# Attention over four 32x32 images: one load queue, rows on other queues, values ahead of the first scores, a quartered end

## The chip, the cores and the metric

The kernel runs on one core of a Trainium2 chip. The metric is the device time of one execution in microseconds, the median of several. The engines are TensorE (PE in the views, its weight loads PEld), VectorE (DVE), ScalarE (ACT), GpSimd (POOL) and SyncE (SP), which only issues transfers here.

## The reference

For each of 4 images of 256 channels and N = 1024 pixels, a block of self-attention with a residual:

```python
xf = x.reshape(B, Cc, N)
q = jnp.einsum('oc,bcn->bon', Wq, xf) + bq[None, :, None]
k = jnp.einsum('oc,bcn->bon', Wk, xf) + bk[None, :, None]
v = jnp.einsum('oc,bcn->bon', Wv, xf) + bv[None, :, None]
scores = jnp.einsum('bqi,bqj->bij', q, k)
attn = jax.nn.softmax(scores, axis=-1)
out = jnp.einsum('bcj,bij->bci', v, attn)
return out.reshape(B, Cc, W, H) + x
```

q and k have 32 channels, v has 256. All is float32.

## The kernel before

Every float32 operand of a product is cut in two: a high part rounded to the format that TensorE reads fast (fp32r), and a low part, the rest. A product of two such operands is three products (high by high, high by low, low by high), which is how `x_hi`, `x_lo`, `wv_hi`, `w_hi`, `w_lo`, `v_hi`, `v_lo` come about. For q and k the parts are stacked on 96 partitions (`q_a`, `k_a`, and copies `q_b`, `k_b`), so one product with 96 rows does all three.

An image passes through four stages. *Projection*: q, k (`project_qk`), and v in 8 pixel tiles of 128 (`v_tile`, six products of 256 columns each). *Scores*: 8 tiles of 128x1024 (`scores`, two products of 512 columns), of which only the row maximum (VectorE, `row_max`) and the sum of exponentials (ScalarE, `sum_exp`) are used. From both comes the shift of each pixel, negative maximum less log of the sum (`shifts`), cut into two parts, transposed into a row by VectorE (`turn_shifts`), and moved by two small transfers (`send_rows`, one for the high and one for the low part) into partitions 96 and 97 of `q_b`; `k_b` has ones there. *Transposed scores*: with these rows, `scores_t` gives the shifted scores transposed, 128 keys by 512 queries, one product per tile; ScalarE's exponential of it (`exp`) is the finished weight, `w_full`. Its high part `w_hi` is made by ScalarE (a second exponential with rounded output) or by VectorE (`cut_w`), its low part `w_lo` by VectorE or GpSimd (`split_w`); `cut_by_act` and `split_by_pool` say by which, from the tile's number. *Weighted sum*: `weigh_v` adds six products of 512 columns per tile into `acc`, two blocks of 128 channels (c = 0, 1). After 8 key tiles one half of the queries (h) is done, and VectorE's `finish` adds bias and residual, channel block by channel block.

A turn of 16 steps (`turn`) does the weighted sums of one image: step s weighs tile s % 8 of half s // 8, while TensorE is two tiles ahead with `scores_t`. Between them the table `FRONT` places the projections and scores of the next image: scores at steps 6 to 13, values from step 5, the last values in step 15. The order on each engine is the order of the code; the engines wait for one another by counting semaphores. PSUM is full: `acc`, `st` (two transposed tiles) and two `slot`s that the front work shares.

The first image has its own start. TensorE runs `keep_busy` products on zeros (fillers) until the data are there, then `first_project_qk`, more fillers, the first four score tiles mixed with the value tiles, `first_rows` (the shifts of the first half turned into a row by products with an identity, `eye_r`, and copied into `q_b` by ScalarE's `put_first_rows`), and the first transposed scores. The homes of these tiles in PSUM are in `FIRST_HOME` and `FIRST_V`. The small weights and the second piece of the first image come over ScalarE's queue, the other loads over SyncE's.

The queues matter for what follows. GpSimd's loop goes through all tiles n; at n % 16 = 8 it issues `k_a` and `q_a` blocks of the next image and the rows of the second half (`send_rows(b, 1)`), at n % 16 = 13 the rows of the next image's first half, and only then subtracts:

```python
if n % PER == JT + 5 and more:
    send_rows(b + 1, 0)
split_w(n)
```

SyncE loads, sends the stacks (`second_stack`) and stores the results.

## Time and profile before

| | |
|---|---|
| median of 3 runs | 168.96 us (168.79 to 169.66) |
| profiled execution | 169.59 us, its span 167.7 us |
| TensorE | busy 160.9 us of the span (96%), 781 matmuls |
| VectorE | 139.1 us (83%) |
| ScalarE | 108.0 us (64%) |
| GpSimd | 47.2 us (28%) |
| transfers | 14.41 MB, 86 GB/s on average |

The span runs from the first recorded event to the last; the execution's own time has 1.9 us more around it. A matmul's recorded duration contains its way through the array, so that of two matmuls in a row overlaps; the distance between their starts is what one costs.

### The profile page before, as it was taken

How to read it: one execution, taken by the hardware profiler on the slowest of the kernel's cores; microseconds unless marked ns; L12 is line 12 of the kernel's file. 1: busy time of each engine (PE TensorE's matmuls, PEld its weight loads, DVE VectorE, ACT ScalarE, POOL GpSimd, SP SyncE). 2: the span in 40 equal slices, each digit the busy share in tenths (PEclk: the TensorE clock that was granted, in tenths of full speed). 3: DMA queues.
4: the chain of work that ended last, by engine and by line, in shares of the span. 5: the costliest groups of instructions: out<-in, count | busy, mean ns of one | idle time of the engine just before them, and what ended most of it. 6: DMA issues, size and time to landing. Idle time of an engine off the chain costs nothing. (4 is left out here: it accounts for less than half of the span.)

```text
span 167.7 us, 2420 instructions
## 1 busy us (share of the span) xinstructions
PE 160.9 (96%) x781; PEld 131.0 (78%) x781; DVE 139.1 (83%) x221; ACT 108.0 (64%) x198; POOL 47.2 (28%) x63
## 2 busy tenths in 40 slices
PE   7898999999999999999999999999999999999992
PEld 4566888797887898788787898788787898876880
DVE  1879889899979999899979998898989879855353
ACT  3667896855997665767896655746896555754410
POOL 4229830080335300340335300250335300203500
PEclk9999999999999999999999999999999999999999
DMA  5923357054311230152310230052310230003003
GB/s 146 390 88 95 68 233 250 0 125 114 127 49 25 69 125 0 34 139 66 125 49 16 83 125 2 16 144 78 124 52 8 89 125 0 4 1 125 0 0 125
DMA packets 7660, 14.41 MB, mean 86 GB/s; under 512 B 1512, under 2 KB 1696, under 8 KB 7648
## 3 DMA queue, kind: packets, MB, share of 16 engines
q1 hardware_dynamic: 6528, 13.11, 23.9%
q0 software_dynamic: 832, 0.82, 2.3%
q10 hardware_dynamic: 288, 0.33, 0.6%
q8 instruction: 6, 0.10, 0.2%
q14 instruction: 6, 0.05, 0.1%
HBM read 4.52 MB, written 4.19 MB: 52 GB/s over the span
## 5 line engine op out<-in xcount | busy, mean ns | idle before, releaser
L826 PE MATMUL acc<-w_hi,v_hi 128*128 128x512 f32 x128 | 51.2, 400 | 0.0
L826 PE MATMUL acc<-w_hi,v_lo 128*128 128x512 f32 x128 | 50.3, 393 | 0.0
L434 ACT ACTIVATE w_full<-st 128x512 f32<-128x512 f32 x64 | 37.8, 593 | 10.5 <-PE st L812 10.5
L401 ACT ACTIVATE dump<-slot,negmax 128x1024 f32<-128x1024 f32 x29 | 32.4, 1118 | 13.2 <-DVE negmax L554 12.9
L834 PE MATMUL acc<-w_lo,v_hi 128*128 128x512 f32 x120 | 38.7, 398 | 0.3 <-POOL w_lo L330 0.2
L609 DVE TENSOR_TENSOR w_lo<-w_full,w_hi 128x512 fp32r<-128x512 f32 x48 | 33.1, 692 | 5.9 <-ACT w_full L434 1.6
L554 DVE TENSOR_REDUCE negmax<-slot 128x1 f32<-128x1024 f32 x29 | 35.3, 1216 | 1.6 <-PE slot L746 1.6
L330 POOL TENSOR_TENSOR w_lo<-w_full,w_hi 128x512 fp32r<-128x512 f32 x16 | 20.7, 1294 | 46.6 <-ACT w_full L434 46.5
L826 PEld LDWEIGHTS acc<-w_hi,v_hi 128*128 128x128 f32 x128 | 24.2, 189 | 7.1 <-DVE x_sb L618 1.2
L826 PEld LDWEIGHTS acc<-w_hi,v_lo 128*128 128x128 f32 x128 | 24.2, 189 | 5.3
L834 PEld LDWEIGHTS acc<-w_lo,v_hi 128*128 128x128 f32 x120 | 22.3, 188 | 7.0 <-POOL w_lo L330 2.0
L812 PE MATMUL st<-q_b,k_b 98*128 98x512 f32 x64 | 25.4, 400 | 0.2 <-issue 0.2
L600 DVE CAST w_hi<-w_full 128x512 fp32r<-128x512 f32 x43 | 21.6, 503 | 4.8 <-ACT w_full L434 4.3
L431 ACT ACTIVATE w_hi<-st 128x512 fp32r<-128x512 f32 x21 | 12.4, 593 | 7.6 <-PE st L812 7.5
L686 PE MATMUL slot<-wv_hi,x_hi 128*128 128x256 f32 x60 | 16.8, 280 | 0.0
L686 PE MATMUL slot<-wv_lo,x_hi 128*128 128x256 f32 x60 | 16.8, 279 | 0.0
L686 PE MATMUL slot<-wv_hi,x_lo 128*128 128x256 f32 x60 | 16.7, 279 | 0.0
L746 PE MATMUL slot<-k_a,q_a 96*128 96x512 f32 x48 | 15.3, 401 | 0.0
L423 ACT ACTIVATE v_hi<-slot 128x512 fp32r<-128x512 f32 x12 | 7.2, 599 | 12.4 <-PE slot L686 12.4
L348 POOL DMA_DIRECT2D q_b<-shift_rows x14 | 8.1, 580 | 21.6 <-DVE shift_rows L582 21.6
L746 PEld LDWEIGHTS slot<-k_a,q_a 96*128 96x128 f32 x48 | 13.1, 310 | 1.4 <-issue 0.4
L812 PEld LDWEIGHTS st<-q_b,k_b 98*128 98x128 f32 x64 | 12.0, 188 | 2.0 <-issue 0.6
(83 smaller groups left out, 188.1 us busy)
## 6 DMA issues: line engine op xcount, KB each, us to landing
out<-x_sb SPq DMA_DIRECT2D x7, 512.0 KB, 2.8
x_sb<-x SPq DMA_DIRECT2D x3, 1024.0 KB, 5.9
k_b<-k_a SPq DMA_DIRECT2D x8, 192.0 KB, 2.5
q_b<-q_a SPq DMA_DIRECT2D x8, 192.0 KB, 2.7
x_sb<-x SPq DMA_DIRECT2D x3, 256.0 KB, 4.2
k_a<-qk_parts SPq DMA_DIRECT2D x12, 64.0 KB, 2.1
q_a<-qk_parts SPq DMA_DIRECT2D x12, 64.0 KB, 2.3
out<-x_sb SPq DMA_DIRECT2D x2, 256.0 KB, 2.1
```

What stands on the lines that cost most here:

```text
L330: nc.gpsimd.tensor_tensor(w_lo[:, r, :], w_full[:, r, :], w_hi[:, r, :].bitcast(fp32), ALU.subtract).then_inc(w_split_pool, 1)
L401: nc.scalar.activation(dump[:, t % 2, :], s_home(b, t), ACT.Exp, bias=negmax[:, t:t + 1], accum_out=rowsum[:, t:t + 1]).then_inc(rowsum_re ...
L431: nc.scalar.activation(w_hi[:, r, :], st[:, j % 2, :], ACT.Exp).then_inc(w_cut_act, 1)
L434: nc.scalar.activation(w_full[:, r, :], st[:, j % 2, :], ACT.Exp).then_inc(exp_done, 1)
L554: nc.vector.tensor_reduce(out=negmax[:, t:t + 1], in_=s_home(b, t), op=ALU.max, axis=AX.X, negate=True).then_inc(negmax_ready, 1)
L600: nc.vector.tensor_copy(w_hi[:, r, :], w_full[:, r, :]).then_inc(w_cut_dve, 1)
L609: nc.vector.tensor_tensor(w_lo[:, r, :], w_full[:, r, :], w_hi[:, r, :].bitcast(fp32), ALU.subtract).then_inc(w_split_dve, 1)
L686: last = nc.tensor.matmul(dst, lhs, rhs, start=(i == 0), stop=(i == len(terms) - 1))
L746: last = nc.tensor.matmul(s_home(b, t)[:, cols(h)], pixels(b, t), k_a[0:K_A, cols(h)], start=True, stop=True)
L812: nc.tensor.matmul(st[:, j % 2, :], k_b[0:K_B, j * P:(j + 1) * P], q_b[0:K_B, cols(h)], start=True, stop=True).then_inc(st_ready, 1)
L826: nc.tensor.matmul(acc[:, c, :], v[:, b % 2, j, ch], w_hi[:, r, :], start=(j == 0 and v is v_hi), stop=False)
L834: last = nc.tensor.matmul(acc[:, c, :], v_hi[:, b % 2, j, c * P:(c + 1) * P], w_lo[:, r, :], start=False, stop=(j == JT - 1))
```

## The change

Six edits in one. (1) All loads are issued by SyncE, the small weights first, then the four pieces of the first image. (2) The rows of the next image's first half are sent by SyncE instead of GpSimd; of the last image's second-half rows ScalarE sends the high part and GpSimd the low part. (3) In the first image GpSimd makes `w_lo` of tiles 3 and 5 (besides 9, 11, 13) and no longer of tile 0. (4) The first two value tiles are computed right behind the projections; their high part is cut by ScalarE, TensorE subtracts it in PSUM by a product with a negative identity, and ScalarE copies what is left as the low part. The other value tiles move up, and the scores of tile 4 ahead of the first transposed product. (5) In the last image the last two steps of each half take channel block 0 of both tiles first, then block 1. (6) In the last half of the last image channel block 1 is summed in two quarters (one in `acc`, one in `slot[0]`), finished and stored separately, one by ScalarE's queue.

```diff
     def split_by_pool(n):
-        return n % PER in (0, 9, 11, 13)
+        return n % PER in ((3, 5, 9, 11, 13) if n < PER else (0, 9, 11, 13))
...
-        FIRST_V = (slot[1][:, cols(1)], st[:, 1, :], slot[0][:, cols(0)], slot[0][:, cols(1)])
+        FIRST_V = (slot[1][:, cols(1)], slot[1][:, cols(1)], st[:, 1, :], slot[0][:, cols(0)])
...
+        def send_rows(engine, b, h, parts=(HI, LO), done=None):
+            engine.wait_ge(shift_turned, 2 * b + h)
+
+            if b:
+                engine.wait_ge(st_ready, PER * (b - 1) + JT * h + JT)
+            for part in parts:
+                engine.dma_start(
+                    q_b[SHIFT + part:SHIFT + part + 1, cols(h)].bitcast(fp32).rearrange("o (q n) -> o q n", n=P),
+                    shift_rows[part:P:SQUARE, h, :]).then_inc(done or row_in[h], DMA)
...
         @block.sync
         def _(sp):
-            for i in (0, 2, 3):
+            sp.dma_start(small_sb[:, :], small).then_inc(small_in, DMA)
+            for i in range(4):
                 c, part = piece(i)
                 sp.dma_start(x_sb[:, 0, c, part], x_v[0, :, c, part]).then_inc(x0_in[i], DMA)
...
                 second_stack(k_b, k_a, 0, kb_in[0])
+                send_rows(sp, b + 1, 0)
                 sp.wait_ge(st_ready, PER * b + PER)
...
-            for c in range(CT):
-                sp.wait_ge(acc_read, 4 * BATCH - 1 + c)
-                sp.dma_start(out_v[BATCH - 1, :, c, cols(1)], x_sb[:, BATCH - 1, c, cols(1)]).then_inc(out_sent[1], DMA)
+            sp.wait_ge(acc_read, 4 * BATCH - 1)
+            sp.dma_start(out_v[BATCH - 1, :, 0, cols(1)], x_sb[:, BATCH - 1, 0, cols(1)]).then_inc(out_sent[1], DMA)
+            sp.wait_ge(acc_read, 4 * BATCH + 1)
+            sp.dma_start(out_v[BATCH - 1, :, 1, quarter(3)], x_sb[:, BATCH - 1, 1, quarter(3)]).then_inc(out_sent[1], DMA)
...
-                    send_rows(b, 1)
+                    send_rows(pool, b, 1, (HI, LO) if more else (LO,))
                     if more:
                         second_blocks(b + 1, 1)
-                if n % PER == JT + 5 and more:
-                    send_rows(b + 1, 0)
                 split_w(n)
...
+            first_cut_v(0)
+            act.wait_ge(v0_rest_ready, 1)
+            nc.scalar.activation(v_lo[:, 0, 0:VT, :], v_home(0, 0).rearrange("p (j c) -> p j c", c=C),
+                                 ACT.Copy).then_inc(v_split, 1)
             for t in range(TH):
                 sum_exp(0, t)
             log_sums(0, 0)
-            first_cut_v(1)
+            first_cut_v(2)
+            first_cut_v(3)
             put_first_rows()
-            first_cut_v(2)
             exp(0)
-            first_cut_v(3)
             exp(1)
...
+                    before, t, image = front(b, s - 2)
+                    if before == S and t == JT - 1 and b + 1 == BATCH:
+                        send_rows(act, b, 1, (HI,), last_row_in)
...
+            def finish_last(i):
+                part = slice(HALF + i * QUARTER, HALF + (i + 1) * QUARTER)
+                if i == 0:
+                    dve.wait_ge(third_quarter_ready, 1)
+                else:
+                    dve.wait_ge(av_done, TILES)
+                nc.vector.scalar_tensor_tensor(
+                    out=x_sb[:, BATCH - 1, 1, part], in0=(slot[0] if i else acc[:, 1, :])[:, 0:QUARTER],
+                    scalar=bv_sb[:, 1:2], in1=x_sb[:, BATCH - 1, 1, part],
+                    op0=ALU.add, op1=ALU.add).then_inc(acc_read, 1)
...
-            split_v(0, 0)
             split_v(0, 1)
             split_v(0, 2)
             row_max(0, TH)
+            cut_w(0)
+            split_w(0)
             split_v(0, 3)
...
+            def weigh_last_tile(h, j, c):
+
+                b = BATCH - 1
+                if c == 0:
+                    weigh_ready(b, h, j)
+                for part, dst in places(h, c):
+                    weigh_high(b, h, j, c, dst, part)
+                    last = weigh_low(b, h, j, c, dst, part)
+                    if (h, j, c) == (1, JT - 1, 1) and part == quarter(0):
+                        last.then_inc(third_quarter_ready, 1)
+                if c:
+                    last.then_inc(av_done, 1)
+                elif j == JT - 1:
+                    last.then_inc(acc0_ready, 1)
...
-            keep_busy(13, QUARTER)
+            keep_busy(14, QUARTER)
             for i in range(4):
                 first_project_qk(i)
-            keep_busy(24, P)
+
+            pe.wait_ge(wv_split, 1)
...
+            for i, (t, xs, w, c) in enumerate(first_v):
+                last = nc.tensor.matmul(v_home(0, 0)[:, t * C:(t + 1) * C], xs[:, 0, c, px[t]], w[:, c, :],
+                                        start=(i == 0), stop=(i == len(first_v) - 1), skip_group_check=True)
+            last.then_inc(v_ready, 1)
+            keep_busy(8, P)
             for t in range(3):
                 first_scores(t)
-            pe.wait_ge(wv_split, 1)
-            v_tile(0, 0)
-            v_tile(0, 1)
+            pe.wait_ge(v_cut, 1)
+            pe.wait_ge(eye_cut, 1)
+            nc.tensor.matmul(v_home(0, 0), eye_r[:, :], v_hi[:, 0, 0:VT, :].rearrange("p j c -> p (j c)"),
+                             start=False, stop=True, skip_group_check=True).then_inc(v0_rest_ready, 1)
+            pe.wait_ge(v_split, 1)
+            v_tile(0, 2)
+            v_tile(0, 3)
             first_scores(3)
```

On ScalarE, between the cuts of the projections and the first exponentials of the scores, the order was this (`k_a`, `q_a` are the projected stacks, `dump` takes exponentials of which only the sum counts):

```order
L454 ACTIVATE q_a<-slot,small_sb 32x512 [waits qk_ready]
L401 ACTIVATE dump,rowsum<-acc,negmax 128x1024 [waits negmax_ready]
L401 ACTIVATE dump,rowsum<-st,negmax 128x1024 [waits negmax_ready]
L401 ACTIVATE dump,rowsum<-slot,negmax 128x1024 [waits rowsum_ready,negmax_ready]
L401 ACTIVATE dump,rowsum<-acc,negmax 128x1024 [waits rowsum_ready,negmax_ready]
L406 ACTIVATE logsum<-rowsum 128x4 [waits rowsum_ready]
L415 ACTIVATE v_hi<-st 128x512 [waits v_ready]
L411 ACTIVATE q_b<-st 2x512 [waits row_ready]
```

In the changed kernel it is this, on the same engine at the same place:

```order
L461 ACTIVATE q_a<-slot,small_sb 32x512 [waits qk_ready]
L422 ACTIVATE v_hi<-slot 128x512 [waits v_ready]
L474 ACTIVATE v_lo<-slot 128x512 [waits v0_rest_ready]
L407 ACTIVATE dump,rowsum<-acc,negmax 128x1024 [waits negmax_ready]
L407 ACTIVATE dump,rowsum<-st,negmax 128x1024 [waits negmax_ready]
L407 ACTIVATE dump,rowsum<-slot,negmax 128x1024 [waits rowsum_ready,negmax_ready]
L407 ACTIVATE dump,rowsum<-acc,negmax 128x1024 [waits rowsum_ready,negmax_ready]
L412 ACTIVATE logsum<-rowsum 128x4 [waits rowsum_ready]
L422 ACTIVATE v_hi<-st 128x512 [waits v_ready]
L422 ACTIVATE v_hi<-slot 128x512 [waits v_ready]
L417 ACTIVATE q_b<-st 2x512 [waits row_ready]
```

Two copies out of PSUM have moved in front of the four exponentials, and a second copy in front of the row's.

On GpSimd, from tile 9 to tile 0 of the next image, the order was (`w_lo` is made, the two transfers to `q_b` are the rows):

```order
L330 TENSOR_TENSOR w_lo<-w_full,w_hi 128x512 [waits av_done,w_cut_act,exp_done] x2
L348 DMA q_b<-shift_rows 1x4x128 [waits st_ready,shift_turned]
L348 DMA q_b<-shift_rows 1x4x128
L330 TENSOR_TENSOR w_lo<-w_full,w_hi 128x512 [waits av_done,w_cut_dve,exp_done]
L330 TENSOR_TENSOR w_lo<-w_full,w_hi 128x512 [waits av_done,w_cut_act,exp_done]
```

Now the two transfers stand on SyncE, between the two halves of `k_b`:

```order
L271 DMA k_b<-k_a 96x512 [waits k_dup_in0,ka_in0,st_ready]
L237 DMA q_b<-shift_rows 1x4x128 [waits st_ready,shift_turned]
L237 DMA q_b<-shift_rows 1x4x128
L271 DMA k_b<-k_a 96x512 [waits k_dup_in1,ka_in1,st_ready]
L271 DMA q_b<-q_a 96x512 [waits q_dup_in1,qa_in1]
```

GpSimd goes from tile 11's subtraction straight to tile 13's.

On TensorE, from the first rows to the first transposed scores (`st`), the order is now:

```order
L824 MATMUL st<-eye_r,shift_parts 2x128 [waits ones_put,eye_cut,shift_ready]
L824 MATMUL st<-eye_r,shift_parts 2x128 x3
L800 MATMUL slot<-k_a,q_a 128x512 [waits v_split,q_lo_put,q_dup_put]
L800 MATMUL slot<-k_a,q_a 128x512
L845 MATMUL st<-q_b,k_b 128x512 [waits kb_in0,qb_in0,row_put]
L845 MATMUL st<-q_b,k_b 128x512 [waits v_split]
L845 MATMUL st<-q_b,k_b 128x512 [waits exp_done]
```

Before, value tile 6 stood between the rows and the first `st<-q_b,k_b`, and the two products of tile 4's scores and value tile 7 behind it.

## Rows read from the trace of the kernel before

**Rows 1.** Chain that ended last, in order of time: start us, us, what.
```profile
134.15 2.80 PE slot L686 x24
...
137.19 0.93 PE acc L826 x4
```

**Rows 2.** Waits: engine, line, waited for: total us, times, longest us.
```profile
PEld acc L834 <- POOL w_lo L330: 2.0, 4, 0.6
```

**Rows 3.** Timeline, third image, step 13: start us, duration us, engine, line, operation.
```profile
127.12 1.16 POOL L348 DMA_DIRECT2D q_b<-shift_rows  x2 [3.18 <-DVE shift_rows L582]
...
128.31 1.31 POOL L330 TENSOR_TENSOR w_lo<-w_full,w_hi 128x512 fp32r<-128x512 f32 x1
...
129.18 0.40 PE L826 MATMUL acc<-w_hi,v_lo 128*128 128x512 f32 x1
...
129.67 0.74 PE L834 MATMUL acc<-w_lo,v_hi 128*128 128x512 f32 x2
```

**Rows 4.** Timeline of TensorE, first image, step 13.
```profile
53.42 0.40 PE L826 MATMUL acc<-w_hi,v_lo 128*128 128x512 f32 x1
...
53.98 0.73 PE L834 MATMUL acc<-w_lo,v_hi 128*128 128x512 f32 x2 [0.16 <-POOL w_lo L330]
```

**Rows 5.** Timeline around the last image's row, steps 5 and 6.
```profile
145.63 1.15 POOL L348 DMA_DIRECT2D q_b<-shift_rows  x2 [12.03 <-DVE shift_rows L582]
...
147.03 0.63 PE L834 MATMUL acc<-w_lo,v_hi 128*128 128x512 f32 x2
...
147.87 0.47 PE L812 MATMUL st<-q_b,k_b 98*128 98x512 f32 x1 [0.21 <-issue]
```

**Rows 6.** DMA issues: transfer, queue, count, KB each, median us to landing.
```profile
k_a<-qk_parts SPq DMA_DIRECT2D x12, 64.0 KB, 2.1
...
out<-x_sb SPq DMA_DIRECT2D x2, 256.0 KB, 2.1
...
q_b<-shift_rows POOLq DMA_DIRECT2D x14, 2.0 KB, 1.6
```

**Rows 7.** Timeline of the start, from the projections to the first weighted sum.
```profile
11.13 1.03 ACT L454 ACTIVATE q_a<-slot,small_sb 32x256 fp32r<-32x256 f32 x2 [0.18 <-DVE q_a L535]
...
11.86 0.50 PE L770 MATMUL acc<-k_a,q_a 96*128 96x512 f32 x1 [0.26 <-DVE k_a L529]
...
12.68 0.63 PE L770 MATMUL slot<-k_a,q_a 96*128 96x512 f32 x2
...
13.66 1.12 ACT L401 ACTIVATE dump<-acc,negmax 128x1024 f32<-128x1024 f32 x1 [1.50 <-DVE negmax L554]
...
14.92 0.73 PE L770 MATMUL acc<-k_a,q_a 96*128 96x512 f32 x2 [0.20 <-ACT dump L401]
...
20.37 0.60 ACT L415 ACTIVATE v_hi<-slot 128x512 fp32r<-128x512 f32 x1
...
20.39 0.50 PE L812 MATMUL st<-q_b,k_b 98*128 98x512 f32 x1
...
23.44 0.73 PE L834 MATMUL acc<-w_lo,v_hi 128*128 128x512 f32 x2
```

**Rows 8.** Timeline of TensorE, first score products of the second image.
```profile
40.06 0.83 PE L746 MATMUL slot<-k_a,q_a 96*128 96x512 f32 x2
```

**Rows 9.** Source line of the `w_hi` casts: duration ns min/median/max, first and last start.
```profile
L600 DVE CAST w_hi<-w_full x43: 405/418/1776, 24.3 to 160.8; 128x512 fp32r<-128x512 f32 x43
```

**Rows 10.** Timeline of TensorE, first projection and first fast one.
```profile
4.73 0.76 PE L713 MATMUL slot<-x_hi,wqk_hi 128*128 128x512 f32 x1 [0.58 <-ACT x_hi L387]
...
8.56 0.40 PE L718 MATMUL slot<-x_lo,wqk_hi 128*128 128x512 f32 x1
```

**Rows 11.** Timeline: a half-width operation at the start, and the end.
```profile
11.84 0.48 DVE L535 SCALAR_TENSOR_TENSOR q_a<-slot,small_sb,q_a 32x256 fp32r<-32x256 f32 x1
...
163.69 1.44 DVE L618 SCALAR_TENSOR_TENSOR x_sb<-acc,small_sb,x_sb 128x512 f32<-128x512 f32 x2 [1.65 <-PE acc L830]
...
163.95 0.39 PE L834 MATMUL acc<-w_lo,v_hi 128*128 128x512 f32 x1
```

More of the change, by code:

```diff
@@ L585, in split_v @@
             def split_v(b, i):
-                if b == 0 and i == 0:
+                if b == 0 and i == 1:
                     dve.wait_ge(v_cut_dve, 1)
@@ new lines, in weigh_high, with weigh_low @@
+            def weigh_high(b, h, j, c, dst, part):
+                n = PER * b + JT * h + j
+                if j == 0 and n:
+                    pe.wait_ge(acc_read, 2 * (2 * b + h) + c - 1)
+                for v in (v_hi, v_lo):
+                    nc.tensor.matmul(dst, v[:, b % 2, j, c * P:(c + 1) * P], w_hi[:, n % RING, part],
+                                     start=(j == 0 and v is v_hi), stop=False)
+            def weigh_low(b, h, j, c, dst, part):
+                n = PER * b + JT * h + j
+                wait_w_split(pe, n)
+                return nc.tensor.matmul(dst, v_hi[:, b % 2, j, c * P:(c + 1) * P], w_lo[:, n % RING, part],
+                                        start=False, stop=(j == JT - 1))
```

106 lines of the change are left out of this document (64 added, 42 removed).

## Prediction

> **What bounds the kernel now.** I read the chain that ended last first. From 128 us to the end it is TensorE on almost every piece, at a steady pace: four 512-column products in 0.93 us, twenty-four 256-column ones in 2.80 us [rows 1]. That is 0.233 us for 512 columns and 0.117 for 256, whatever the tile. From the first weighted sum on, the span is the number of columns times that pace, plus whatever TensorE stands still. So for each edit I ask which standstill it takes away or adds. Next I read the waits and, around each, the timeline, where a standstill is the distance of two starts less the pace.
>
> In the steady part one line of the waits stands out: weight loads of the low part waited for GpSimd's `w_lo` in four places [rows 2]. At the third image's step 13 the timeline shows why. GpSimd first issues the two row transfers of the next image (from 127.12, 1.16 us) and only then does the subtraction (128.31 to 129.62). The product that needs it starts at 129.67, 0.49 after the last one instead of 0.23, and the pair then takes 0.74 where others take 0.63 [rows 3]: 0.26 + 0.11 = 0.37 us. In the first image the same place costs 53.98 - 53.42 - 0.23 = 0.33 and 0.10 [rows 4]; the second image repeats the third. **Together 1.17 us in three images.** In the last image a row for its own second half costs once more: two transfers are issued one behind the other from 145.63 on, 1.15 us in all; 1.6 us after the second issue (146.2) it lands, near 147.8; the score product starts at 147.87 where the pace would have had it at 147.50, and lasts 0.47 instead of 0.40 [rows 5, 6]: 0.44 us.
>
> Ahead of the first weighted sum TensorE does not set the pace; a chain over four engines does. The first exponential starts at 13.66 behind VectorE's first row maximum, four of them at 1.1 us follow, then logs and row, the first transposed score product at 20.39, and the first low-part product at 23.44 [rows 7].
>
> **The change, part by part.**
>
> *Next image's rows from SyncE instead of GpSimd.* The two transfers are on SyncE's queue now, behind `k_b`'s first half and ahead of its second. At step 13 GpSimd starts 1.16 us sooner and ends near 128.5, while the product wants the result at 129.41: the stall goes with 0.9 us to spare, **-1.17 us**. Behind the transposed rows SyncE queues `k_b`'s second half, which isn't due before the image's last score product, later than the transpose; nobody waits for it sooner. The row lands, by the 2.1 us that a SyncE transfer of 64 KB takes [rows 6], at 127.1 + 0.6 + 2.1 = 129.8 at the latest. It is wanted after the pair at 129.67 and two score products of 0.47 us together, less the 0.37 saved, at 130.35. Cover 0.5 us; the bounds of the landing are 1.6 us (this transfer from GpSimd) and 2.1.
>
> *Last image's row, one part from ScalarE and one from GpSimd.* They no longer stand in line. GpSimd's lands at 145.63 + 1.6 = 147.2, ScalarE's, issued about then, between 147.0 and 147.7; wanted at 147.50. **-0.40 us** (-0.2 if ScalarE's takes 2.1). The Trainium skill ("DMA: Bandwidth & Descriptors", "Latency and other measured facts") gives a hardware queue's first byte about 0.6 us and GpSimd's about 1. No row here separates the two; by it ScalarE's part would not be the later one, and the term is -0.44. ScalarE now waits for the transpose ahead of two exponentials, which slip by about 1.2 us. Followed through the timeline, they still come a few tenths (an estimate) before TensorE wants the cut of tile 7 in the new order. I count nothing, but this cover is thin; if it is gone, the 0.40 goes too.
>
> *Low parts 3 and 5 of the first image to GpSimd, 0 to VectorE.* VectorE is relieved of two subtractions ahead of late row maxima, GpSimd has no other work there. The pair of score products at 40.06 took 0.83 instead of 0.63 [rows 7, 8]: a late stack of the second image, whose parts come out of this VectorE queue. **-0.20 us** (0 to -0.37). Against it: a cast of `w_hi`, 0.42 us at the median, took up to 1.78 [rows 9]. The Trainium skill ("SBUF — State Buffer", "SBUF: two separate sides") says that VectorE and GpSimd share a port pair which the first to start locks for its whole instruction; that cast agrees. Worked out from rows, two more subtractions of 1.3 us on GpSimd [rows 3] could hold VectorE for up to 2.6 us in the first image. VectorE's row maxima read the scores from PSUM and it is near idle behind the fourth of them, so I take nothing.
>
> *First image's values ahead of the scores.* Two tiles' twelve products (1.40 us) and 8 fillers stand where 24 fillers stood. The first score product moves to about 11.4, but its second half waited for `k_lo` until 11.86, so nothing is lost. Then ScalarE, free from 12.16 to 13.66 [rows 7]. It now copies the values' high part (12.2 to 12.8, at 0.60 a copy), waits for the product with the negative identity, and copies the low part. That product stands behind the score products that started at 12.68 and ended at 13.31, so it ends near 13.55, and the first exponential starts near 14.1: +0.45. Tiles 2 and 3 (1.40 us) may start only when the low part is out, and the fourth pair of scores stands behind them: 14.2 + 1.5 = 15.7 instead of 14.92, so that the fourth exponential is 0.6 late. Last, the scores of tile 4 now stand ahead of the first transposed product and wait for a `v_lo` of VectorE behind the shifts: 20.39 becomes 21.0. From there to the first low-part product it was 3.05 us. 1.17 of that was the last value tile and the scores of tile 4, now ahead, but the third transposed product still waits for both exponentials of the first tile; I take 2.9, so 23.9 instead of 23.44. **+0.50 us** for the block (0.2 to 0.8, the ends from ScalarE's delay alone counted half and from each delay added in full). Moved work is not saved: the same columns pass before 23.44, and one 512-column product more.
>
> *Loads in one row.* The first piece of x is issued one issue later, behind the small weights, about 0.4 us, but no longer shares the transfer engines with a second queue; the second piece comes sooner. TensorE's first projection stood at 4.73 and lasted 0.76; from 8.56 on they last 0.40 [rows 10]. Up to there it is at its low level and nearly without gaps. **-0.10 us** (-0.4 to +0.4: one issue time, either way).
>
> *The end.* Channel block 0 is finished 1.40 us before the last product instead of 0.70, block 1 in two quarters. Before, VectorE took both blocks from 163.69 in 1.44 us, to 165.13, the last product ending at 164.34. Half the width took 0.48 where 0.74 is the whole [rows 11]. So the last quarter is done at 164.39 + 0.48 = 164.87, 0.26 less, and 128 KB land a little sooner than 256 KB in 2.1 us [rows 6]. **-0.30 us** (0.2 to 0.4). The quarters carry the same columns at the same pace [rows 1]; they cost nothing.
>
> **Sum**: -1.17 - 0.40 - 0.20 + 0.50 - 0.10 - 0.30 = -1.67, and 0.1 (0 to 0.3) for the hand-over between the last image's halves, whose first block is read earlier too: -1.8 us. The profiled execution took 169.59 with a span of 167.7; it would be 167.8 with a span of 165.9. The median shown, 168.96, is 0.63 under that execution, so I predict 167.1.
>
> **Rivals.**
> *The start gains too.* If the loads give 0.4 us and ScalarE's copies fit their 1.5 us of idle, the start gives 0.4 instead of taking it: 166.3. Against it stands the product's place behind 13.31.
> *VectorE takes the place.* With `w_lo` on time, VectorE may be what TensorE meets next, above all if the lock bites in the first image. Then 1.17 and 0.20 stay out: 168.5. Against it: TensorE waited for VectorE nowhere in the steady part by more than tenths, and an early subtraction frees VectorE's blocked cast.
> *Slower: TensorE's clock rises later.* The gap between fillers and first projection may grow. Were the low level kept past 8.56 until the first transposed scores are near, the remaining projections, 1.40 us of values and 1.9 us of scores would take twice as long and push the whole chain by 2.6 us or more: +0.8, 169.8. It decides from 1.8 us of added chain on; below 1 us the forecast holds.
> *The middle does nothing:* SyncE's row lands over 0.5 us late and TensorE waits at step 14 for what it no longer waits at 13: 168.3.
>
> **Chances.** Forecast 0.60, start gains 0.15, VectorE 0.12, middle 0.06, clock 0.07. About 0.5% (0.85 us) is what a measurement here tells from no change. Faster by that: the first two and half of the fourth, 0.78; within: 0.14; slower: 0.08. The likeliest case alone spans 166.2 to 168.1 by its bounds; the range, with its neighbours, 165.9 to 168.6.
>
> **What would show it.** GpSimd's `w_lo` of step 13 right behind its cast and no TensorE wait there; the last image's score product within 0.1 of its pace; the first exponential near 14.1, the first transposed score product near 21.0, the first low-part product near 23.9; the last VectorE operation ending 0.5 us behind the last product. What would make me wrong: a first exponential at 13.7, a first projection past 5.3, or new TensorE waits for VectorE.

## The result, and the profile after

Seven executions of the changed kernel took 169.33 to 171.12 us, median 170.54, beside 168.97 for the kernel before (7 executions). The ratio is 1.006, 95% interval 1.003 to 1.009: 0.6% slower, where 1.1% faster was forecast; the two medians alone are 0.9% apart. (In all ratios below, executions over 1.5% above the fastest of their kernel are left out; medians and counts take all.)

The profiled execution took 171.12 with a span of 169.0; that of before 169.59 with 167.7. By core, the span and the mean granted clock of TensorE in the changed kernel:

```profile
core 0: 169.0 us, clock 0.990
```

Six of the seven show a mean of 0.99; the seventh, at 1.00, took 169.33. The mean doesn't say where the clock was low. The windows of the changed kernel, TensorE alone (columns: busy us and instructions, granted clock, share of the transfer engines, GB/s):

```profile
21.00:22.00 1.00, 0.82 (x3) 1.00 0.70 131
22.00:23.00 1.00, 0.47 (x3) 1.00 1.03 401
23.00:24.00 1.00, 0.59 (x3) 1.00 0.95 369
24.00:25.00 1.00, 1.00 (x4) 0.62 0.34 127
25.00:26.00 1.00, 1.00 (x4) 0.50 0.07 29
26.00:27.00 1.00, 1.00 (x4) 0.50 0.00 0
27.00:28.00 1.00, 1.00 (x4) 0.68 0.91 111
28.00:29.00 1.00, 1.00 (x6) 1.00 1.04 426
```

The recorded clock is 1.00 everywhere else. It fell to half, the lower of its two levels (1.2 GHz of 2.4), from 24.2 to 27.6 us, just as the weighted sums began. The timeline shows what that is to a product, and what came ahead:

```profile
23.41 0.50 PE L845 MATMUL st<-q_b,k_b 98*128 98x512 f32 x1 [0.94 <-ACT w_full L441]
23.75 0.40 PE L858 MATMUL acc<-w_hi,v_hi 128*128 128x512 f32 x1
...
24.61 0.63 PE L858 MATMUL acc<-w_hi,v_lo 128*128 128x512 f32 x1
25.04 1.06 PE L864 MATMUL acc<-w_lo,v_hi 128*128 128x512 f32 x2
26.74 0.63 PE L845 MATMUL st<-q_b,k_b 98*128 98x512 f32 x1
```

Starts are 0.43 us apart for 512 columns instead of 0.23, and the third transposed score product had waited 0.94 us for the first tile's exponential: TensorE was busy 0.82, 0.47 and 0.59 us of the three before. In the kernel before it was busy 1.00 in each of the windows from 20 to 25 us.

The start, answering to [rows 7, 10]:

```profile
5.14 0.77 PE L743 MATMUL slot<-x_hi,wqk_hi 128*128 128x512 f32 x1 [0.77 <-ACT x_hi L393]
...
13.78 0.39 PE L935 MATMUL slot<-v_hi,eye_r 128*128 128x512 f32 x1
14.21 0.60 ACT L474 ACTIVATE v_lo<-slot 128x512 fp32r<-128x512 f32 x1 [1.07 <-PE slot L935]
14.83 1.12 ACT L407 ACTIVATE dump<-acc,negmax 128x1024 f32<-128x1024 f32 x1
...
16.38 0.63 PE L800 MATMUL acc<-k_a,q_a 96*128 96x512 f32 x2
...
21.18 0.83 PE L800 MATMUL slot<-k_a,q_a 96*128 96x512 f32 x2 [0.29 <-DVE v_lo L605]
21.84 0.63 PE L845 MATMUL st<-q_b,k_b 98*128 98x512 f32 x2
```

First exponential 14.83 (13.66 before, 14.1 forecast), fourth scores 16.38 (14.92), first transposed product 21.84 (20.39, forecast 21.0), first low-part product 25.04 (23.44, forecast 23.9).

Step 13 of the third image, answering to [rows 3]:

```profile
128.80 1.15 SPq L237 DMA_DIRECT2D q_b<-shift_rows  x2
...
129.16 1.29 POOL L349 TENSOR_TENSOR w_lo<-w_full,w_hi 128x512 fp32r<-128x512 f32 x1 [3.28 <-PE acc L864]
...
130.09 0.65 DVE L615 CAST w_hi<-w_full 128x512 fp32r<-128x512 f32 x1
...
131.13 0.39 PE L858 MATMUL acc<-w_hi,v_lo 128*128 128x512 f32 x1
131.36 0.64 PE L864 MATMUL acc<-w_lo,v_hi 128*128 128x512 f32 x2
```

SyncE issues the rows while GpSimd subtracts, from 129.16 to 130.45. The pair that stalled at 129.67 in the kernel before is the one at 131.36 here: it follows at its pace, 0.23 after the last high part, 0.9 us after the subtraction's end, as forecast. The last image's row, answering to [rows 5], and the end, answering to [rows 11]:

```profile
146.94 1.06 ACTq L237 DMA_DIRECT2D q_b<-shift_rows  x1
...
147.20 0.59 POOL L237 DMA_DIRECT2D q_b<-shift_rows  x1 [12.00 <-DVE shift_rows L597]
...
148.11 0.60 ACT L438 ACTIVATE w_hi<-st 128x512 fp32r<-128x512 f32 x1 [1.76 <-PE st L845]
...
148.60 1.08 ACT L441 ACTIVATE w_full<-st 128x512 f32<-128x512 f32 x2
...
149.25 0.19 PEld L845 LDWEIGHTS st<-q_b,k_b 98*128 98x128 f32 x1 [0.46 <-ACT w_full L441]
...
165.74 0.28 PE L864 MATMUL slot<-w_lo,v_hi 128*128 128x256 f32 x1
166.10 0.48 DVE L633 SCALAR_TENSOR_TENSOR x_sb<-slot,small_sb,x_sb 128x256 f32<-128x256 f32 x1
166.60 0.34 SPq L312 DMA_DIRECT2D out<-x_sb  x1
```

A ruler for all that follows: each kernel has the same 64 transposed score products, and the start of the n-th (n from 0) less that of the kernel before tells where time is won or lost. Worked out from the timelines of the profiled executions (old_start+loads is after_old_start_loads below):

```
 n   before  changed  start_only  start_fill  rows_sp  no_act_row  old_start+loads  pool_set  pool_six  finish_first
 0    20.39    +1.45       -0.07       -0.08    +0.11       +0.22            -0.67     -0.79     -0.58         -0.64
 2    22.14    +1.27       -0.26       -0.25    +0.11       +0.21            -0.66     -0.78     -0.59         -0.64
 4    26.58    +2.67       +1.08       -0.41    +0.10       +0.23            -0.67     -0.13     -0.59         -0.65
 8    38.27    +2.63       +1.04       -0.45    +0.12       +0.23            -0.65     -0.17     -0.63         -0.63
 9    40.73    +2.27       +0.68       -0.81    +0.14       +0.23            -0.64     -0.53     -0.82         -0.58
15    52.49    +2.38       +0.78       -0.71    +0.15       +0.24            -0.64     -0.42     -0.82         -0.57
16    55.02    +1.95       +0.78       -0.71    -0.27       -0.18            -1.06     -0.85     -1.24         -0.99
26    80.62    +1.95       +0.78       -0.71    -0.28       -0.19            -1.07     -0.85     -1.25         -1.00
27    82.95    +2.29       +0.77       -0.71    +0.05       +0.17            -0.71     -0.51     -0.90         +0.28
32    92.87    +1.94       +0.76       -0.70    -0.30       -0.18            -1.07     -0.87     -1.26         -0.08
48   130.73    +1.57       +0.76       -0.72    -0.68       -0.56            -1.44     -1.25     -1.64         -0.46
55   145.87    +1.56       +0.76       -0.73    -0.69       -0.57            -1.45     -1.26     -1.65         -0.47
58   151.21    +1.61       +0.75       -0.72    -0.66       -0.53            -1.37     -1.19     -1.59         -0.40
63   159.76    +1.64       +0.76       -0.71    -0.66       -0.44            -1.27     -1.10     -1.49         -0.32
```

So the 1.3 us of the changed kernel's span are: +1.27 by n = 2, +1.40 in the stretch of the low clock, -0.29 up to n = 15, -1.16 at the three stalls of step 13 (-0.43, -0.35, -0.38), +0.34 between 26 and 27, +0.07 from 48 to 63, and -0.35 behind.

One caution for all columns. TensorE's first rise to its fast pace comes at another moment in each execution of one and the same kernel. In the kernel before 512 columns of the first projections take 0.43 us up to 8.56 us [rows 10]; in rows_sp, whose start is the same, they do up to the last of them at 9.72, and in start_fill they take 0.23 from 7.22 on. That moves n = 0 by up to 1 us, and the end with it. The executions of the kernel before, too, nearly all lie in two groups, 168.6 to 169.1 and 169.4 to 170.1, and a median falls now in the one and now in the other. Below 0.3 us, therefore, I read the ruler and not the medians.

### The profile page after: what moved, and what is told of

Read it like the earlier page. It is cut to its first block, busy times and chain, and to the rows that moved or that the text cites. A ratio compares the mean times of both kernels' runs of the same rounds, so it can differ in the third digit from the quotient of the medians.

```text
span 169.0 us, 2445 instructions
## 1 busy us (share of the span) xinstructions
PE 161.4 (96%) x791; PEld 133.7 (79%) x791; DVE 136.0 (80%) x220; ACT 109.0 (65%) x199; POOL 44.4 (26%) x57
## 4 chain that ended last, share of the span: by engine, by line
PE 88%; DVE 5%; DMA 2%; ACT 2%; issue 1%; DVEq 0%; SPq 0%; ACTq 0%
PE acc L858 34%; PE acc L864 17%; PE slot L716 11%; PE st L845 9%; PE slot L776 6%; DMA x_sb<-x 2%; PE slot L800 2%; PE slot L733 2%; PE slot L728 2%; DVE negmax L569 1%; PE slot L743 1%; PE slot L746 1%; PE slot L748 1%; PE slot L858 1%; DVE v_lo L605 1%
## 5 line engine op out<-in xcount | busy, mean ns | idle before, releaser
L858 PE MATMUL acc<-w_hi,v_hi 128*128 128x512 f32 (+1 forms) x128 | 50.7, 396 | 0.3 <-DVE x_sb L648 0.2
L858 PE MATMUL acc<-w_hi,v_lo 128*128 128x512 f32 (+1 forms) x128 | 49.6, 389 | 0.0
L864 PE MATMUL acc<-w_lo,v_hi 128*128 128x512 f32 (+1 forms) x128 | 41.3, 392 | 0.0
L349 POOL TENSOR_TENSOR w_lo<-w_full,w_hi 128x512 fp32r<-128x512 f32 x17 | 22.4, 1319 | 68.9 <-ACT w_full L441 38.9
L864 PEld LDWEIGHTS acc<-w_lo,v_hi 128*128 128x128 f32 x128 | 23.9, 190 | 5.6 <-DVE w_lo L624 0.5
L615 DVE CAST w_hi<-w_full 128x512 fp32r<-128x512 f32 x43 | 18.6, 433 | 6.2 <-ACT w_full L441 5.8
L716 PE MATMUL slot<-wv_hi,x_hi 128*128 128x256 f32 x56 | 15.7, 281 | 0.7 <-ACT v_lo L474 0.7
L716 PE MATMUL slot<-wv_lo,x_hi 128*128 128x256 f32 x56 | 15.6, 279 | 0.0
L716 PE MATMUL slot<-wv_hi,x_lo 128*128 128x256 f32 x56 | 15.6, 279 | 0.0
L648 DVE SCALAR_TENSOR_TENSOR x_sb<-acc,small_sb,x_sb 128x512 f32<-128x512 f32 x15 | 10.7, 744 | 2.4 <-PE acc L864 2.4
```

The lines of the kernel that those rows point to most:

```text
L349: nc.gpsimd.tensor_tensor(w_lo[:, r, :], w_full[:, r, :], w_hi[:, r, :].bitcast(fp32), ALU.subtract).then_inc(w_split_pool, 1)
L615: nc.vector.tensor_copy(w_hi[:, r, :], w_full[:, r, :]).then_inc(w_cut_dve, 1)
L716: last = nc.tensor.matmul(dst, lhs, rhs, start=(i == 0), stop=(i == len(terms) - 1))
L858: nc.tensor.matmul(dst, v[:, b % 2, j, c * P:(c + 1) * P], w_hi[:, n % RING, part], start=(j == 0 and v is v_hi), stop=False)
L864: return nc.tensor.matmul(dst, v_hi[:, b % 2, j, c * P:(c + 1) * P], w_lo[:, n % RING, part], start=False, stop=(j == JT - 1))
```

## The experiments

Twelve executions of each, and 29 or 35 of the kernel before on the same chip. The theory was that the middle gains as forecast and the start costs more, through a late chain and a fall of the clock; its rivals that the loads, the rows' new places or the end are to blame.

**rows_sp: the rows of the next image on SyncE alone.** The kernel before and

```diff
-                if n % PER == JT + 5 and more:
-                    send_rows(b + 1, 0)
                 split_w(n)          # GpSimd
                 second_stack(k_b, k_a, 0, kb_in[0])
+                send_rows(sp, b + 1, 0)
```

> The kernel before with one edit: the rows of the next image's first half on SyncE instead of GpSimd. If the stall at step 13 is worth what the rows said, 0.37 to 0.43 us in each of three images, the time is 1.1 to 1.2 us below before, no TensorE wait for w_lo of tiles 13, 29 and 45 is left, and the first transposed product of each next image comes at its pace. If VectorE or the row's landing takes the place of the stall, a new wait stands at step 14 or 15 and the gain is under 0.4 us.

168.9 against 169.7; ratio 0.995 (0.994 to 0.997). The ruler gives -0.42, -0.35 and -0.38 at the three stalls, 1.15 in all. But between n = 26 and 27 it takes 0.33 back, and the second stall's gain only makes up for that. In its timeline:

```profile
78.92 1.22 DVE L554 TENSOR_REDUCE negmax<-slot 128x1 f32<-128x1024 f32 x1
80.05 1.40 DVE L618 SCALAR_TENSOR_TENSOR x_sb<-acc,small_sb,x_sb 128x512 f32<-128x512 f32 x2
80.34 0.40 PE L812 MATMUL st<-q_b,k_b 98*128 98x512 f32 x1
...
80.94 0.47 PE L826 MATMUL acc<-w_hi,v_hi 128*128 128x512 f32 x1 [0.20 <-DVE x_sb L618]
```

At the second image's change of halves VectorE takes a row maximum and then `finish`, at 78.92 and 80.05 as before (78.85 and 79.98). TensorE, 0.28 earlier now (80.34 for 80.62), waits for it: 0.60 between two starts, where it was 0.25.

**loads: the loads in one row alone.** `small` and the second piece of x leave ScalarE's queue for SyncE's.

> The kernel before with one edit: all loads on SyncE in one row. If the loads are behind the late start of the changed kernel, the first projection starts at about 5.1 instead of 4.7, TensorE reaches its high level about 2 us later than before, the first exponential starts 0.4 to 0.7 us later and the time is 0.3 to 0.7 us above before. If the loads were harmless and only the values ahead of the scores cost, the time is within 0.2 us of before.

169.74, ratio 1.000 (0.998 to 1.002). In its profiled execution, which was the longest of its twelve (170.27), the first projection came at 5.48 instead of 4.73, and the ruler stands at +0.70 from the first landmark to the last:

```profile
5.48 0.77 PE L712 MATMUL slot<-x_hi,wqk_hi 128*128 128x512 f32 x1 [1.33 <-ACT x_hi L386]
```

**after_old_loads: the changed kernel with the old loads.**

> The changed kernel with the loads of before (small weights and second piece on ScalarE's queue). Theory: the start of the changed kernel is late by about 0.4 to 0.7 us through its loads and by 0.7 to 1.0 through the values ahead of the scores, and TensorE's fall to the low level after its idle stretch near 22 to 23.4 costs 1.2 more, wholly apart from the loads: then this kernel is 0.4 to 0.7 us below the changed one and its granted clock still falls near 24. Rival: the fall comes from the late start alone; then the granted clock stays at its high level here and the time is 1.5 to 2 us below the changed one.

168.25, ratio 0.995 (0.992 to 0.998). Seven of twelve at 167.98 to 168.28 with a clock of 0.997 or more, five at 169.55 to 171.05 with 0.99. The same kernel, two times.

**after_fill: the changed kernel with nine products on zeros.** In TensorE's idle stretch, into a bank that is free there:

```diff
             pe.wait_ge(v_split, 3)
             scores_t(1)
+            for i in range(9):
+                nc.tensor.matmul(acc[:, 0, 0:P], idle[:, 0:P], idle[:, 0:P], start=True, stop=True)
```

> The changed kernel with nine 128-column fillers (0.5 us of work) between the second and the third transposed score product, into a place of PSUM that the first weighted sum overwrites. The third product waits for ScalarE there anyway, so they cost no time themselves. If the fall of TensorE's clock at 24.2 comes from the idle stretch ahead of it, the granted clock stays high from 24 to 28 and the time is 1.0 to 1.5 us below the changed kernel. If the fall has another cause, the time is that of the changed kernel within 0.3 us.

168.58, ratio 0.996 (0.993 to 0.998), no execution of twelve at 0.99. **after_again**, the changed kernel itself on another chip, shows how much hangs on that:

> The changed kernel itself again, on the same chip as the run with the fillers beside it, since its 7 runs were taken elsewhere. If the fall of the clock belongs to the kernel: 8 or more of 12 executions with a mean granted clock of 0.99, median 170.2 to 170.8. If it belonged to the chip or the hour of those 7 runs: about as many as in the run with the fillers, median near 168.8.

169.27 against 169.0, ratio 0.999 (0.996 to 1.002); one execution of twelve at 0.99 (171.37), and one of 171.75 whose clock reads 1.00, so that not every long execution shows a low mean. The kernel that was 0.6% slower in its seven executions is no slower in these twelve. Its profiled execution, of 170.03, has the same waits ahead of the first weighted sum and kept its clock:

```profile
21.00:22.00 1.00, 0.71 (x6) 1.00 1.02 158
22.00:23.00 1.00, 0.82 (x4) 1.00 0.85 315
23.00:24.00 1.00, 0.24 (x1) 1.00 1.01 381
24.00:25.00 1.00, 1.00 (x5) 1.00 0.59 234
```

The waits, then, are not sufficient. **fill_early** has the nine products ahead of the first scores (`keep_busy(17, P)` for 8):

> The changed kernel with the same nine products of 128 columns put elsewhere: ahead of the first scores, where TensorE has eight such already. If it is the idle stretch of TensorE at 20 to 24 us on which the clock falls: it falls here too, median 170.2 to 170.9 (up to 0.5 later if the scores wait for the nine). If nine more products anywhere, or the changed phase of the work, keep the clock up: 168.4 to 168.8 as with the nine in the idle stretch.

169.53, ratio 1.002 (0.999 to 1.006), three of twelve at 0.99, and those took 170.87 to 171.95: between the two theories, and not telling by itself.

**start_only and start_fill: the new start alone, without and with the nine products.** The kernel before with the values ahead, the negative identity and the new set of GpSimd's tiles.

> The kernel before with the new start alone (values ahead, negative identity, first image's tiles 3, 5, 9, 11, 13 on GpSimd); loads, rows of scores and end as before. Theory A (the start costs 0.5 to 0.8 by later first products, 1.2 more in the executions where the granted clock falls between 24 and 28 us, and gives 0.4 back on the second image's stack): the timed runs split, those without the fall within 0.3 of before, those with it 1.2 to 1.5 longer; median 169.8 to 171. Rival (the start gains what its author could want, and the loss comes from its meeting with the loads in one row alone): 168.8 to 169.3 and no fall.

> The kernel before with the new start alone, and the nine products of 128 columns between the second and third transposed product of scores. Without them 9 of 12 executions had a mean granted clock of 0.99 and took 170.5 to 172. If the idle stretch of TensorE just ahead is what the clock falls on: at most 2 of 12 with 0.99, median 168.8 to 169.4. If the executions fall for another reason of the new start and the nine only helped where the loads and rows were changed too: 6 or more of 12 with 0.99, median above 170.

170.65 with nine of twelve at 0.99 (170.49 to 171.96); the three others 168.96 to 169.26. With the nine products 169.06 and none at 0.99, on another chip. Since the changed kernel's share had differed between chips, both ran again, side by side on one chip (start_only_2, start_fill_2):

> The new start alone, a second time, on the same chip as the next two. If the fall of the clock is the kernel's: 6 or more of 12 executions with a mean granted clock of 0.99, median above 170. If its frequency is the chip's or the hour's: fewer, and the median within 0.3 of before.

> The new start alone with the nine products in the idle stretch, beside the run without them. If they hold the clock up: at most 1 of 12 at 0.99 whatever the run beside it shows, median within 0.2 of before. If the chip decides: the same share as the run beside it.

170.41 with seven of twelve at 0.99, and 169.03 with none: of all pairs with and without the products this is the one on the same chip. The two profiled executions of the first pair have the same start to 0.01 us. start_only:

```profile
20.32 0.63 PE L816 MATMUL st<-q_b,k_b 98*128 98x512 f32 x2
21.88 0.79 PE L816 MATMUL st<-q_b,k_b 98*128 98x512 f32 x1 [0.94 <-ACT w_full L435]
22.47 0.63 PE L830 MATMUL acc<-w_hi,v_hi 128*128 128x512 f32 x1
22.90 0.63 PE L830 MATMUL acc<-w_hi,v_lo 128*128 128x512 f32 x1
```

start_fill:

```profile
20.31 0.64 PE L816 MATMUL st<-q_b,k_b 98*128 98x512 f32 x2
20.79 0.68 PE L883 MATMUL acc<-idle 128*128 128x128 bf16 x9
21.89 0.50 PE L816 MATMUL st<-q_b,k_b 98*128 98x512 f32 x1 [0.42 <-ACT w_full L435]
22.22 0.40 PE L830 MATMUL acc<-w_hi,v_hi 128*128 128x512 f32 x1
22.46 0.39 PE L830 MATMUL acc<-w_hi,v_lo 128*128 128x512 f32 x1
```

The third transposed product comes at the same moment in both; behind it one goes at 0.43 a product and the other at 0.23. By n = 4 they are 1.08 + 0.41 = 1.49 us apart, and stay so to the end. Over all kernels with the new start, 31 of 67 executions without the products in that stretch had 0.99, and with them 1 of 48.

A mean of 0.99 alone is not this fall. The kernel before shows it too, in 6 of 163 executions beside these runs, and rows_sp, pool_set and finish_first in one of twelve each; those took 168.99 to 169.91, and all but pool_set's lie within the times of the others of their kernel.

**old_start_idle: an idle stretch in the old start.** after_old_start_loads (below), in which TensorE waits for the second exponential ahead of the first weighted sum (`pe.wait_ge(exp_done, 2)` behind `scores_t(1)`).

> The kernel before with the new places of the rows and the new end (ratio 0.9944 in its run, no fall in 12), with the old start, in which TensorE waits for the second tile's exponential ahead of the first weighted sum, so that it stands idle for about 1.8 us at 21.7 to 23.5. If an idle stretch there is what the clock falls on, whatever the start: several of 12 executions at 0.99, and those 1.2 to 2.8 longer than the others; without a fall 1.5 to 1.8 longer than its own kernel, 169.7 to 170. If the fall needs the new start's order: none at 0.99, all within 169.7 to 170.8.

170.21; three of twelve at 0.987 to 0.989, but at 170.06 to 170.69 no longer than the others. In its profiled execution TensorE stood still throughout 23 to 24 us, and the clock held:

```profile
22.00:23.00 1.00, 0.70 (x5) 1.00 1.06 434
23.00:24.00 1.00, 0.00 (x0) 1.00 0.96 393
24.00:25.00 1.00, 0.87 (x4) 1.00 0.01 0
```

So one idle stretch of 1.4 us was not enough in this execution. Neither forecast came true: some executions did show a low mean, down to 0.987, the lowest of all, but they were no longer, and where their clock was low isn't recorded. Whether an idle stretch in the old start brings a fall on stays open.

**after_old_start and after_old_start_loads: the new rows and end with the old start,** with the new loads and with the old.

> The changed kernel with the start of the kernel before (values after the scores, plain identity, the old sets of tiles, the old order on every engine of the start); the loads stay in one row, the rows on SyncE, the last image's row on ScalarE and GpSimd, the new end. Theory A (the new start is what costs, by the later first products and by the clock's fall that it brings on): three stalls of the second row gone (about -1.1, with some 0.35 given back at the hand-over of the second image) and the end -0.4, so 167.9 to 168.3 against 169.7 before, and no fall of the granted clock. Theory B (the loads in one row cost 0.7 in every kernel that has them): 168.8 to 169.2. Theory C (something else in the middle of the changed kernel costs, the rows' new places or the end): no gain, 169.5 to 170.

> As the run before, with the loads of the kernel before as well, so the kernel before with the new places of the rows and the new end alone. Theory A: the same as with the new loads within 0.3, 167.9 to 168.3. Theory B: 0.5 to 0.7 shorter than with the new loads, since they come sooner. Theory C: 169.5 to 170.

168.74, ratio 0.996 (0.993 to 0.999), and 168.19, 0.994 (0.992 to 0.997); no execution of the 24 at 0.99.

**no_act_row: the last image's row from GpSimd alone again,** in the second of them.

> As the run before, with both parts of the last image's second row put out by GpSimd, as before. If the issue on ScalarE won nothing, because its own 1.06 us delay the next exponentials that TensorE then waits for: equal within 0.15. If it won the 0.40 that the prediction gave it: 0.4 longer. If the delay also hurts the hand-over to the last half: up to 0.2 shorter.

168.96, ratio 0.996 (0.994 to 0.999). Its median falls in the upper group and isn't telling; the ruler is. From n = 55 to 58, across the row, this kernel goes from -0.57 to -0.53, the one with ScalarE's issue from -1.45 to -1.37, and the changed kernel from +1.56 to +1.61. The stall of [rows 5] is there in no_act_row (0.42 us short of the pace) and gone in the other, but that one has four others of 0.09 to 0.20 behind the late exponentials.

**old_loads_fill: both repairs in the changed kernel.**

> The changed kernel with the loads of the kernel before and with nine products of 128 columns between the second and the third transposed score product, both repairs together. If the fall of the clock and the late loads are two separate costs: the gains add, 168.25 less about 1.0, so 167.0 to 167.5, granted clock 1.0 throughout. If the loads only mattered through the clock (a later start widens the idle stretch): about that of the fill alone, 168.3 to 168.6.

168.22, ratio 0.995 (0.992 to 0.998), one of twelve at 0.99. That is after_fill's ratio again and not 167.0 to 167.5: with the clock kept up, the old loads add nothing that shows.

**pool_set and pool_six: the set of tiles.** In after_old_start_loads:

```diff
-        return n % PER in (0, 9, 11, 13)
+        return n % PER in ((3, 5, 9, 11, 13) if n < PER else (0, 9, 11, 13))     # pool_set
+        return n % PER in ((0, 3, 5, 9, 11, 13) if n < PER else (0, 9, 11, 13))  # pool_six
```

> The kernel before with the new places of the rows and the new end (168.19 in its run), and the first image's tiles 3, 5, 9, 11, 13 subtracted on GpSimd in place of 0, 9, 11, 13. If the 0.36 that the changed kernel gained before its ninth transposed product of scores is this edit's: 0.36 less at that landmark, 0.2 to 0.4 shorter in all. If it is the new start's, by a shift of phase: 0, or up to 0.3 longer since VectorE has tile 0 to do at the start.

168.94. The ruler gives 0.36 between n = 8 and 9, as in the changed kernel, and takes 0.65 between 2 and 4. There VectorE has tile 0 now:

```profile
23.31 0.74 PE L862 MATMUL acc<-w_lo,v_hi 128*128 128x512 f32 x2 [0.59 <-DVE w_lo L622]
```

> The kernel before with the new places of the rows and the new end (168.19 in its run), and tiles 3 and 5 of the first image added to GpSimd's 0, 9, 11 and 13, with none taken away. The set that gave tile 0 back to VectorE showed TensorE waiting 0.59 for that tile's low part at 23.31, and 0.35 to 0.41 less at the ninth landmark. If the two are separate: the wait at 23 us is gone, the later gain stays, and the whole is 0.3 to 0.4 shorter than without, 167.8 or so, the fastest here. If GpSimd's six tiles run into its cuts of the second image: new waits of TensorE for GpSimd near tiles 3 to 5, no gain.

168.21 against 169.0, ratio 0.993 (0.991 to 0.996), the lowest of all ratios, with the fastest single execution, 167.20. The loss at tile 0 is gone, and of the gain 0.19 is left at n = 9 and 0.23 from n = 4 to 15. It is the version to keep: the kernel before with the rows on SyncE, the last image's row shared with ScalarE, the new end, and six tiles on GpSimd. The times don't tell it from after_old_start_loads (168.19, 0.994, on another chip); that tiles 3 and 5 help rests on the ruler.

**finish_first: `finish` ahead of the row maximum** at the second image's change of halves, for the 0.34 lost there.

> The kernel before with the new places of the rows and the new end, and at the second image's change of halves VectorE adds to the outputs first and takes the row maximum that stood ahead of it afterwards. If the 0.35 that every kernel with the rows on SyncE gives back at this place is VectorE's order (the maximum of 1.22 us ahead of the additions): that stall of TensorE goes, -0.35 at the next landmark, 0.2 to 0.4 shorter. If the maximum's delay of 1.4 holds ScalarE's sums and the slot that the next scores go to: a new wait of up to 1 us at the next scores, and no gain or a loss.

169.75, ratio 1.002 (0.999 to 1.005): a loss of 1.28 at that place in place of 0.34. The wait for `finish` is gone, so it was VectorE's order that set it: the weighted sum starts at 79.86, 0.24 after the product before it. But ScalarE's sum, behind the later maximum, holds the slot that the next scores go to:

```profile
81.28 1.11 ACT L408 ACTIVATE dump<-slot,negmax 128x1024 f32<-128x1024 f32 x1 [2.23 <-DVE negmax L567]
...
82.53 0.86 PE L777 MATMUL slot<-k_a,q_a 96*128 96x512 f32 x2 [1.11 <-ACT dump L408]
```

## Why the prediction was wrong, point by point

**The step that failed** is "+0.50 us for the block (0.2 to 0.8)" for the values ahead. It summed delays of a chain at TensorE's fast pace, and did not ask what the added wait ahead of the third transposed product does to that pace. Two things came out otherwise.

The fall of the clock, which the forecast didn't have, costs 1.5 us in the executions that show it (start_only and start_fill, 1.49; +1.40 in the changed kernel); with it alone 1.8 us less becomes 0.3 less. And the delay is 0.5 us only where the projections end early: start_fill, in which they end at 8.6 us, reaches n = 4 at 26.17, and pool_six, in which they end at 8.9, at 25.99, so 0.2 + 0.3 = 0.5 us. Where they end late it is more: old_loads_fill (10.35) and after_fill (10.5) reach n = 4 at 27.61 and 28.00, rows_sp (10.15) at 26.68, which is 0.7 and 1.0 when their later end is taken off. In the profiled execution of the changed kernel they ended at 10.4 instead of 9.5.

The forecast, 1.8 us less, and that execution's span, 1.3 more, are 3.1 us apart. The fall is 1.4 of them; the start up to n = 2 is 0.9 (+1.27 where block and loads were to give +0.50 - 0.10); the last image's row 0.5; the hand-over 0.4; tiles and end gave 0.1 more than forecast. With the clock held up the whole is 0.4% faster (after_fill), 0.7 us instead of 1.8, so the fall is not all that was missing.

The rival "TensorE's clock rises later" had the right mechanism at another place: it looked at the first rise and gave "from 1.8 us of added chain on"; what decided was a fall at a time that the forecast took for steady. The Trainium skill ("TensorE: Matmul & The Clock Gate", "HAM oscillation — how this bites in real kernels") describes TensorE dropping to its low rate in waits between bursts of products. By the windows above the trace agrees that the fall follows a stretch with waits; but after_again waited as much and old_start_idle stood still for 1.4 us in one piece, and both kept their clock in the profiled execution, so the rule doesn't tell here which execution falls.

*Rows on SyncE, -1.17:* right, -1.16 in the changed kernel and -1.15 alone.

*Hand-over, -0.1:* wrong in place and sign. It stood for the last image; the second image's costs +0.34, since VectorE's order sets that moment. This is the rival "VectorE takes the place", true at one of three places.

*Last image's row, -0.40:* nothing, +0.05. The working said that "this cover is thin; if it is gone, the 0.40 goes too". It was gone: the issue on ScalarE took 1.06 us where GpSimd's took 0.59, and so the next exponential began at 148.11, 1.76 after the end of the one before it, though its scores had left TensorE at 146.2; then TensorE waited for ScalarE (149.25). I had counted the wait and not the issue.

*Tiles 3 and 5, -0.20:* -0.23 to -0.30 between n = 4 and 15, rightly placed at the second image's stack. Not priced was tile 0 on VectorE, 0.65 in the old start (pool_set); in the new start tile 0's cut and low part stand ahead of the last value part, and no such loss shows (start_fill, -0.25 to -0.41). The lock between VectorE and GpSimd, taken at nothing, cost TensorE nothing that shows. It is there: the cast of 1.78 us in [rows 9] ran from 128.13 beside GpSimd's subtraction (128.31 to 129.62) and ended 0.29 after it, and in the changed kernel, where the subtraction ends earlier beside it, the cast takes 0.65 and again ends 0.29 after it. That the first to start holds the pair isn't what the records show here, in which the cast starts first.

*Loads, -0.10 (-0.4 to +0.4):* alone nothing measurable. The first projection, for which "past 5.3" was named as a sign against the forecast, came at 5.14 in the profiled execution. Over all profiled executions with the new loads it came at 4.70, 4.75, 5.14, 5.48, 5.80 and 6.26; with the old ones, fourteen in all, at 4.59 to 4.81 and once at 5.06. So the single row of loads often brings it late, which the term didn't have. Beside the old start the old loads are 0.5 faster by the medians, which the two groups of executions leave uncertain; the sign is a loss, if anything.

*End, -0.30:* -0.35 in the profiled execution (from n = 63 to the end 7.55 us instead of 7.90), but not in all. VectorE's last operation is about 0.16 earlier in every kernel with the new end. The last transfer then took 1.89 to 1.90 us in eight of thirteen profiled executions (pool_set and pool_six among them), and 2.11 to 2.20 in the other five (among them no_act_row, 7.88, and after_old_start_loads, 7.90), against 2.04 in the kernel before: there the end gave 0.10 or less. Why is open. Added to the rows it moved no median that I could tell.

What stays open: what decides whether the clock falls. The same kernel had it in 6 of 7 and in 1 of 12 executions, the start alone in 9 and 7 of 12. That the nine products at that place keep it up is shown by one pair on one chip (7 of 12 and 0 of 12) and fits the counts of the others; that the idle stretch is its whole cause is not shown, since after_again had it and kept its clock, and old_start_idle didn't bring about the loss.

## What to carry to other kernels

Where an edit at the start leaves TensorE waiting in short pieces, read the granted clock by windows over the next microseconds, in several executions: a delay of 0.5 us can bring 1.5 behind it, and a few products on zeros in the gap, where their bank is free, delayed nothing here (21.89 and 21.88) and went with 1 such execution in 48 instead of 31 in 67. A transfer issued from an engine on the path costs that engine its whole issue, not only its wait (here 1.06 us). When a stall goes, look which engine's own order comes next; it takes part of the gain, and turning that order round can cost more than it gave.

## What the runs showed of the hardware

In the changed kernel the granted clock reads 1.00 from 3 to 10 us, while 512 columns take 0.43 us, about twice the later 0.23; only the distance of the starts tells the level there. The moment of the change differs by some 5 us between executions of one and the same start: in after_old_start_loads the second projection product, at 5.06, already lasts 0.40; in rows_sp the one at 9.72 still lasts 0.63. A later change need not cost its whole delay, since other engines bound that stretch too: the projections of rows_sp end 0.6 us after those of the kernel before, and its first transposed product comes 0.11 after.

Later, the recorded clock of one kernel fell to 0.50 in one profiled execution (24.2 to 27.6 us) and stayed at 1.00 in another, after waits of about the same size (changed kernel and after_again).

The issue of one row of 2 KB took 1.06 us on ScalarE's queue and 0.59 on GpSimd's; two took 1.15 on SyncE's. It isn't ScalarE's queue as such: its issue of the last image's output quarter took 0.38.

A cast on VectorE beside a subtraction on GpSimd ended 0.29 us after it, both where it took 1.78 us and where it took 0.65.
